# Two 128x128 transposes per pair moved from TensorE to VectorE's 32x32 blocks and SBUF-to-SBUF transfers

## What is computed

```python
base = jnp.einsum('btd,od->bto', x, W)
logits = jnp.einsum('btd,ed->bte', x, Wr) + one_hot(ids) * 5.0
topw, topi = jax.lax.top_k(logits, 2)
gates = jnp.sum(one_hot(topi) * softmax(topw)[..., None], axis=-2)
h = jnp.einsum('btd,erd->bter', x, A)                 # 8 experts, rank 16
c = base + 2.0 * jnp.einsum('bter,bte,eor->bto', h, gates, B)
weight = U * S[None, :] @ V.T                         # 1024 x 256 x 1024
out = x + jnp.einsum('bti,oi->bto', c, weight)
```

## Time and profile before

| | |
|---|---|
| runs of the kernel before, us | 154.99, 155.07, 155.89 (median 155.07) |
| the profiled execution, us | 155.31 |
| its span, from the first instruction to the last, us | 153.5 |
| busy: PE, DVE, POOL, ACT, us | 148.2, 106.6, 71.2, 63.5 |
| DMA traffic | 32.72 MB, mean 213 GB/s |

### The profile page before, as it was taken

How to read it: one execution, slowest core, us unless ns; L and a number is a source line. 1 busy time by engine, 2 the same in 40 slices (tenths; PEclk the granted TensorE clock), 3 DMA queues, 4 the chain that set the end, 5 groups by cost and what they waited for, 6 DMA issues and landing times.

```text
span 153.5 us, 2910 instructions
## 1 busy us (share of the span) xinstructions
PE 148.2 (97%) x1056; PEld 139.3 (91%) x1056; DVE 106.6 (69%) x297; ACT 63.5 (41%) x141; POOL 71.2 (46%) x56
## 2 busy tenths in 40 slices
PE   7999999999999999899999999999999999999991
PEld 5899989999999988898999899989999998998880
DVE  0776896769578999948674875587559746785951
ACT  3576877884636423346204611361334104013000
POOL 2000233992660666582866196627664640631800
PEclk9999999999999999999999999999999999999999
DMA  5999999999104040069509912990482068006184
GB/s 169 364 386 414 399 409 411 410 406 411 70 4 137 0 137 0 4 255 352 212 19 361 384 62 97 351 367 11 179 265 107 0 260 273 19 0 273 68 334 144
DMA packets 10669, 32.72 MB, mean 213 GB/s; under 512 B 1440, under 2 KB 1952, under 8 KB 10528
## 3 DMA queue, kind: packets, MB, share of 16 engines
q1 hardware_dynamic: 10368, 31.96, 55.4%
q10 hardware_dynamic: 288, 0.59, 1.0%
HBM read 24.16 MB, written 8.39 MB: 212 GB/s over the span
## 4 chain that ended last, share of the span: by engine, by line
PE 80%; DMA 6%; DVE 5%; SPq 4%; issue 2%; DVEq 1%; ACT 0%
PE fin L334 10%; PE pj L335 9%; PE pj L334 9%; PE fin L336 9%; PE fin L335 9%; PE pj L336 9%; PE zt L336 6%; PE zt L334 6%; PE zt L335 6%; DMA xt_raw<-in_xt 6%; SPq L197 2%; DVE w_lo L713 2%; SPq L220 1%; PE gt L418 1%; PE zt L405 1%
## 5 line engine op out<-in xcount | busy, mean ns | idle before, releaser
L281 POOL TENSOR_TENSOR xT_lo<-xt_raw,xT_hi 128x1024 fp32r<-128x1024 f32 x16 | 38.4, 2404 | 40.9 <-ACT xT_hi L582 21.2
L296 POOL TENSOR_TENSOR x_all<-x_all,vw_raw 128x512 f32<-128x512 f32 x21 | 26.6, 1298 | 28.2 <-DVE vw_raw L818 26.3
L334 PE MATMUL pj<-proj_hi,xT_hi 128*128 128x264 f32 x128 | 36.9, 288 | 0.0
L335 PE MATMUL pj<-proj_lo,xT_hi 128*128 128x264 f32 x128 | 36.3, 284 | 0.0
L336 PE MATMUL pj<-proj_hi,xT_lo 128*128 128x264 f32 x128 | 36.2, 283 | 0.0
L334 PE MATMUL fin<-v_hi,w_hi 128*128 128x256 f32 (+1 forms) x88 | 28.1, 320 | 0.2 <-DVE w_lo L713 0.2
L335 PE MATMUL fin<-v_lo,w_hi 128*128 128x256 f32 (+1 forms) x88 | 27.9, 317 | 0.0
L336 PE MATMUL fin<-v_hi,w_lo 128*128 128x256 f32 (+1 forms) x88 | 27.9, 317 | 0.0
L335 PEld LDWEIGHTS pj<-proj_lo,xT_hi 128*128 128x128 f32 x128 | 24.1, 189 | 0.2
L334 PEld LDWEIGHTS pj<-proj_hi,xT_hi 128*128 128x128 f32 x128 | 24.1, 188 | 0.2
L336 PEld LDWEIGHTS pj<-proj_hi,xT_lo 128*128 128x128 f32 x128 | 24.0, 188 | 0.0
(11 more groups left out here) (93 smaller groups left out, 272.6 us busy)
## 6 DMA issues: line engine op xcount, KB each, us to landing
xt_raw<-in_xt SPq DMA_DIRECT2D x16, 512.0 KB, 7.4
x_all<-in_x SPq DMA_DIRECT2D x16, 512.0 KB, 6.5
out<-x_all SPq DMA_DIRECT2D x13, 512.0 KB, 3.1
vw_raw<-in_VW SPq DMA_DIRECT2D x6, 384.0 KB, 8.0
w_raw<-in_W SPq DMA_DIRECT2D x8, 256.0 KB, 7.4
out<-x_all SPq DMA_DIRECT2D x5, 256.0 KB, 2.0
w_raw<-in_U SPq DMA_DIRECT2D x1, 1024.0 KB, 6.9
aw_raw<-in_AW SPq DMA_DIRECT2D x1, 544.0 KB, 8.1
```

The source lines that it names most:

```text
L281: nc.gpsimd.tensor_sub(xT_lo[:, t % XTR, :, :], xt_raw[:, t % XTR, :, :], xT_hi[:, t % XTR, :, :].bitcast(F32)).then_inc(xt_lo, 1)
L296: nc.gpsimd.tensor_add(x_all[:, t % XR, cols], x_all[:, t % XR, cols], ups[:, j, :]).then_inc(side_add, 1)
L334: nc.tensor.matmul(dst, l_hi, r_hi, start=first, stop=False, skip_group_check=shared)
L335: nc.tensor.matmul(dst, l_hi, r_lo, start=False, stop=False, skip_group_check=shared)
```

## The change

In pairs 1 to 6 TensorE does no transposes. turn_z(t), within the gates of a tile, has DVE transpose the 32x32 blocks of z's first half from pj into blk, and turn_gh(p) does it for gh. That leaves the sixteen blocks transposed in themselves but in the wrong places. The four on the diagonal are copied by ACT (move_diagonal); the other twelve are each moved by one DMA on SP (move_blocks): 32 partitions, four matrices (gh and z of two tiles), 32 columns of 4 bytes, so 16 KB. The result is tr. blk, tr and zs lie in w_raw, which is free by then. From tr gh is split by split_gh_moved on ACT and DVE, and sums adds z's half from tr to zt, before its four additions. There is no split_za any more: all seven blocks go through zs and are split at once by split_zb, 896 columns instead of 640. half_t writes to zt in even pairs and to gt in odd ones. mix(p) for p from 1 to 6 moves from project(2p+2) to project(2p+3). Pairs 0 and 7 keep the transposes on TensorE. POOL's first split_x is issued in two halves.

```diff
             for p in range(1, PAIRS):
...
+                if p < PAIRS - 1:
+                    move_blocks(p)
                 if p >= 2:
                     store_pair(p - 2)
...
+            def move_blocks(p):
+                sp.wait_ge(blk_done, 3 * p)
+                for i in range(SQS):
+                    for j in range(SQS):
+                        if i != j:
+                            sp.dma_start(tr[SQ * j:SQ * (j + 1), p % 2, :, SQ * i:SQ * (i + 1)],
+                                         blk[SQ * i:SQ * (i + 1), p % 2, :, SQ * j:SQ * (j + 1)]).then_inc(tr_load, 16)
...
-                    if t >= 2 and t % 2 == 0 and k == MH:
+                    if t == 2 and k == MH:
+                        mix(0)
+                    if t >= 5 and t % 2 == 1 and k == MH:
                         mix(t // 2 - 1)
...
-                    if k == MH + 1:
-                        pe.wait_ge(z_copied, 2 * p + 2)
+                    if k == MH + 1 and (p == 0 or p == PAIRS - 1):
+                        pe.wait_ge(z_copied, 2 if p == 0 else 4)
...
             def p1(p):
-                pe.wait_ge(za_lo, p + 1)
                 if p == 0:
+                    pe.wait_ge(za_lo, 1)
                     pe.wait_ge(us_lo_done, 1)
+                else:
+                    pe.wait_ge(zb_lo, p + 1)
...
                 half_t(p)
-                transpose_gh(p)
+            transpose_gh(PAIRS - 1)
...
+            def copy_half(p):
+                act.wait_ge(zt_done, p + 1)
+                act.wait_ge(zb_lo, p)
+                nc.scalar.copy(zs[:, 1:3, :], zt_v[p % 2][:, 1, :, :]).then_inc(z_half_copied, 1)
...
+            def split_gh_moved(p):
+                act.wait_ge(tr_load, MOVES * p)
+                act.wait_ge(tr_diag, SQS * p)
+                nc.scalar.copy(ghT_hi[:, :], tr[:, p % 2, 0:2, :]).then_inc(gt_hi, 1)
+
+            def move_diagonal(p):
+                act.wait_ge(blk_done, 3 * p)
+                for i in range(SQS):
+                    rows = slice(SQ * i, SQ * (i + 1))
+                    nc.scalar.copy(tr[rows, p % 2, :, rows], blk[rows, p % 2, :, rows]).then_inc(tr_diag, 1)
...
+            def turn_z(t):
+                nc.vector.transpose(blk[:, (t // 2) % 2, 2 + t % 2, :], pj[t % 2][:, Z0:TCOLS]).then_inc(blk_done, 1)
+
+            def turn_gh(p):
+                dve.wait_ge(gh_done, 2 * p + 2)
+                nc.vector.transpose(blk[:, p % 2, 0:2, :], gh[:, :, :]).then_inc(blk_done, 1)
...
             def sums(p):
                 n = 4 * p
-                nc.vector.tensor_add(zs[:, 1, :], zt_v[:, 0, 1, :], zs[:, 0, :]).then_inc(sums_done, 1)
+                dve.wait_ge(zt_done, p + 1)
+                dve.wait_ge(tr_load, MOVES * p)
+                dve.wait_ge(tr_diag, SQS * p)
+                dve.wait_ge(z_half_copied, p)
+                nc.vector.tensor_add(zs[:, 0:8:7, :], zt_v[p % 2][:, 0, :, :], tr[:, p % 2, 2:4, :]).then_inc(z0_done, 1)
+                dve.wait_ge(z0_done, p)
+                nc.vector.tensor_add(zs[:, 3, :], zs[:, 7, :], zs[:, 2, :]).then_inc(sums_done, 1)
...
             def pair_2():
                 split_zb(0)
                 split_us(1)
-                split_za(1)
                 up(0, 1)
                 up(0, 2)
+                split_gh_moved(1)
+                xb1(0)
+                gates(4)
                 sums(1)
-                gates_top(4)
-                gates_apply(4)
-                xb1(0)
+                gates(5)
+                turn_gh(2)
                 xa0(0)
-                gates_top(5)
-                gates_apply(5)
                 xb0(0)
                 xa1(0)
-                split_gh(2)
+                split_zb(1)
```

More of the change, by code:

```diff
@@ L622, in split_gh @@
             def split_gh(p):
[L623 to L624 removed]
+                act.wait_ge(gt_done, 1 if p == 0 else 2)
+                nc.scalar.copy(ghT_hi[:, :], (gt if p == 0 else pj[0])[:, 0:2 * P]).then_inc(gt_hi, 1)
             def copy_z(t):
@@ L636, in pair @@
                     split_x(2 * p + 2)
-                split_za(p - 1)
-                copy_x22(p - 1)
                 copy_u(p - 2)
-                copy_z(2 * p)
+                if p == 2:
+                    split_gh_moved(1)
+                if p == PAIRS - 1:
+                    copy_z(2 * p)
                 exp_top(2 * p)
-                split_zb(p - 1)
                 if p < PAIRS - 1:
                     split_x(2 * p + 3)
-                copy_z(2 * p + 1)
+                if p >= 3:
+                    split_gh_moved(p - 1)
+                copy_half(p - 1)
+                split_zb(p - 1)
+                if p == PAIRS - 1:
+                    copy_z(2 * p + 1)
                 exp_top(2 * p + 1)
-                split_gh(p)
+                if p < PAIRS - 1:
+                    move_diagonal(p)
+                else:
+                    split_gh(p)
             first = RANK + P
@@ L908, in _ @@
             split_za(0)
-            sums(0)
-            gates_top(2)
-            gates_apply(2)
-            gates_top(3)
-            gates_apply(3)
+            sums_first()
+            gates(2)
+            gates(3)
+            turn_gh(1)
             split_t(1)
-            split_gh(1)
             pair_2()
```

143 lines of the change are left out of this document (92 added, 51 removed).

## The result

The changed kernel takes 165.45 us (median of 6 runs, 164.18 to 166.32), the kernel before 155.22 in the same six rounds: ratio 1.065, 95% interval 1.0602 to 1.0698. The forecast was 154.9 with a range of 152.3 to 159.9; the change is slower by 6.5%. The profiled execution took 165.8 us around a span of 164.0, against 155.31 around 153.5.

What follows compares the result with a forecast made beforehand. TensorE bounds the kernel, busy 97% of 153.5 us. Transposes -2.6, xb1 wait -0.8, new waits +0.7 and +2.7 sum to 0.0, taken as -0.2 after carrying through by pair: 154.9 us, range 152.3 to 159.9.

Steps and rivals of the forecast that it cites:

- The issue step: SP's twelve moves per pair: 0.47 us from one issue to the next, the last issued 5.2 us after the first.
- Rival C: Moves land late in each pair, so the mix is 1.0 us late in pairs 3 to 7: 159.9 us; chance 0.24.
- the knee: ghT_hi later than POOL's first side addition ends (S+7.5), thus landing over 7.6 us after turn_gh; DVE then held until S+8.8.
- The bound of 180: Slow bound of the moves, 13.5 us from turn_gh to last landing: mix some 5 us late five times, 180 us.
- The lock: While POOL works on SBUF, a DVE instruction with two SBUF inputs waits until POOL's instruction ends; 2.7 us in pair 3.
- The stop at p1(1): PE at p1(1), due at 67.6, waits 2.7 us for split_zb(1), held by split_x(7) on POOL and ending at 70.3.
- from pair 3 on ... I count no wait: Later pairs: DVE done at S+7.8 for a mix due S+8.1, split_zb at S+2.5, due S+2.9; no PE wait.
- The transposes: PE's transposes of z and gh in pairs 1 to 6 go: 6 x 0.44 = 2.6 us saved.
- rival D: half_t's z transposes were free in the shadow of weight loads: gain 1.3 us less, 156.2 us; chance 0.05.
- xb1: Pair 2: xb1(0) now ahead of the gates of tile 4, so PE's wait of 0.8 us at p3(0) goes.
- The landing of 1.8: Each 16 KB move lands 1.8 us after its issue, taken from smallest stores landing in 1.8 to 2.4 us.
- Pairs of 14.1: PE's new pair without the transposes takes 14.1 us; pairs 4 to 6 were to show 14.1 each.

Runs made afterwards that it cites:

- Without the chain: Changed kernel with six of twelve moves left out, 156.82 us; or with one DMA a pair replacing moves and diagonal copies, blocks not placed, 156.88 us.
- the ceiling of 2.3: Kernel before with xb1(0) moved forward (154.12 us), TensorE's gh and z transposes in pairs 1 to 6 left out, nothing in their place: 151.81 us.
- light split: Changed kernel with one DMA a pair, GpSimd's split of the x tiles of pairs 3 to 7 cut to one of eight chunks: 152.87 us.
- the run with ten: Changed kernel with six of the twelve moves done as ScalarE copies beside the four diagonal ones, six left to DMA: 161.46 us.
- the run with contiguous moves: Changed kernel, its twelve moves and diagonal copies each of one contiguous 128-column piece a partition, blocks not put in place: 165.33 us.
- one transfer: Changed kernel with one 128x512 DMA per pair in place of twelve moves and four diagonal copies, blocks not put in place: 156.88 us.
- three tries: GpSimd's split put behind its residual adds with two issuing queues (163.85 us) or one DMA (162.69); held until gh in the version through HBM (158.98).

## Why the prediction was wrong, point by point

**The issue step failed.** The prediction put 0.47 us from one issue to the next, "as most issues stand near 0.43", and its landing at 7.0 us after turn_gh. Those rows were loads from HBM. Between two places in SBUF, of which the trace of before has no row, it is 0.60 + 0.04. Eleven steps of 0.64 and 1.8 of landing give 8.9 us where 7.0 was put, as measured in most pairs, and the irregular steps of two pairs make it 9.8 there. The mixes waited 9.7 us in all, in place of 0.7.

**Rival C is what happened, by its mechanism, not by its price.** It named its point (a step of 0.53) and its place, the mix of every pair; but it was priced at the point itself, 5 us, and the range ended there, at 159.9. Put 0.64 into the same working and the landing lies 1.9 us later than the forecast has it, 1.3 past the knee: ghT_hi 8.8 after the start, ghT_lo 9.3 where nothing holds it, against a mix due at 8.1; five or six times 1.2, so 161 to 162. An estimate of what stands above that: 1.9 us that are missing from the forecast even without the chain, and 0.9 in each of the two pairs with irregular steps, which together come near the 165.45. The hold by POOL's second side addition, which C had in its working, shows in one pair alone (ghT_lo took 1.13 us; 0.43 to 0.79 in the others). The bound of 180 stood beside it and was not taken into the range. A chance of 0.24 for C was too little for a step that had no row of its own kind.

**The lock cost more than the one stop.** Without the chain (156.82 and 156.88) the kernel is still 1.9 us above the forecast of 154.9. The stop at p1(1) is 2.0, forecast 2.7. But "from pair 3 on ... I count no wait" failed: 0.5 us a pair. The split that the working places, ending at +1.5, did end there (+1.7). The other split of the pair, which it leaves out, ended at +5.0 and held dtop by 1.1 us, and ghT_lo came at +8.5 and not +7.8, against a mix due at +8.1. Only the two rows stood for the lock, and I placed POOL's instructions in pair 2 with care and in later pairs by one number. With the split made light the time is 152.87: the lock costs 4.0 us, more than the ceiling of 2.3.

**What held.** The transposes: 2.3 us measured, 2.6 forecast, so rival D (1.3) is out. xb1: 1.0 for 0.8. The turns (row by row: 128x128 with a step of about 0.23, 128x256 about 0.4; forecast 0.2 and 0.4):

```profile
L819 DVE STREAM_TRANSPOSE w_raw<-pj x12: 308/309/311, 46.6 to 131.7; 128x128 f32<-128x128 f32 x12
...
L823 DVE STREAM_TRANSPOSE w_raw<-gh x6: 445/446/446, 49.6 to 132.8; 128x256 f32<-128x256 f32 x6
```

The landing of 1.8. Pairs of 14.1, where nothing is late (14.15 in the light split). The four diagonal copies took 1.26 us rather than 0.75, past their upper bound of 1.1, and cost nothing here; their neighbours in the run with ten did. In the changed kernel the stop at p1(1) is only 0.2 us. PE had stopped for 2.5 us at mix(1) just before, but so it had in the run with contiguous moves, which waited 1.5 at p1(1) still. The difference is TensorE's clock: in the changed kernel it was low between the two, PE came later by itself, and the same lateness of VectorE was hidden behind that.

**The sum, as the runs give it**, from 155.2: the transposes -2.3, xb1 -1.0, the lock +4.0, and what is left up to the 156.88 of one transfer, +1.0 (the p1(1) wait of 0.7 that stays with a light split, and what the runs don't separate); then the chain of twelve issues, with whatever the low clock behind its stops costs, +8.6. That is 165.5.

## What to carry to other kernels

Price an issue by a row of the same kind, from the same side to the same side; where there is none, a chain of a dozen turns an error of 0.17 us into 2 us, and its bound belongs in the range. Work moved off TensorE onto VectorE must be placed against GpSimd's long instructions, one by one and in each pair: it isn't VectorE's busy share (71%) that tells whether it is in time, but which of its small steps meets a 2.4 us instruction of GpSimd, and shifting that instruction only chooses another victim (three tries, all slower). Before replacing something, leave it out: 2.3 us was all that the transposes had to give.
